# Decoder layer on one core: the last values projection, the first turns, the last mergings and a gate tile change places in TensorE's order

## What is computed

```python
x = layernorm(x + self_attn(x))           # 32 heads of 16, causal, with biases
x = layernorm(x + cross_attn(x, ctx))     # 32 query heads of 128, 8 key/value heads, rotary q and k
x = layernorm(x + ffn(x))                 # silu(x Wg) * (x Wu), then Wd; 4-bit weights, 1376 wide
```

```python
q = rope(heads(query @ wq)); k = rope(heads(ctx @ wk)); v = heads(ctx @ wv)
w = softmax(mask(q k^T / sqrt(128)))      # 4 query heads share one k/v head
out = merge_heads(w v) @ wo
```

## Time and profile before

| what | value |
|---|---|
| median of three runs | 888.88 us (887.12 to 889.69) |
| the profiled execution: its time | 887.8 us |
| the profiled execution: its span, first to last instruction | 885.9 us |
| mean granted clock of TensorE in it | 0.993 |
| TensorE busy | 95% of the span |
| VectorE busy | 82% of the span |

### The profile page before, as it was taken

How to read it: one execution, slowest core, us unless ns; L and a number is a source line. 1 busy time by engine, 2 the same in 40 slices (tenths; PEclk the granted TensorE clock), 3 DMA queues, 4 the chain that set the end, 5 groups by cost and what they waited for, 6 DMA issues and landing times.

```text
span 885.9 us, 17326 instructions
## 1 busy us (share of the span) xinstructions
PE 841.4 (95%) x6141; PEld 470.2 (53%) x6141; DVE 726.9 (82%) x1129; ACT 497.2 (56%) x1487; POOL 590.0 (67%) x522
## 2 busy tenths in 40 slices
PE   8898999889799999999999999999999899999897
PEld 4666777555445555555555555554555544333343
DVE  5589998877777888879788788798899764899887
ACT  5787889443555555556565565654654652777400
POOL 1264449886647775776677677578788642887885
PEclk9999999999999999999999999999999999999999
DMA  6765245203134413314224215113622412330011
GB/s 181 232 202 161 73 132 163 66 1 120 25 90 126 107 36 85 86 46 132 61 37 120 61 36 153 38 25 87 141 74 41 101 31 71 96 129 3 1 48 47
DMA packets 119893, 76.75 MB, mean 87 GB/s; under 512 B 72861, under 2 KB 104064, under 8 KB 119808
## 3 DMA queue, kind: packets, MB, share of 16 engines
q1 hardware_dynamic: 117504, 74.99, 31.3%
q10 hardware_dynamic: 2304, 0.66, 0.3%
HBM read 52.50 MB, written 6.36 MB: 66 GB/s over the span
## 4 chain that ended last, share of the span: by engine, by line
PE 51%; POOL 15%; DVE 14%; issue 7%; ACT 7%; DMA 4%; SPq 0%; ACTq 0%; DVEq 0%; POOLq 0%
PE bank L359 14%; PE bank L360 14%; PE bank L361 14%; POOL rot L630 3%; DVE total L1305 2%; DMA pT<-pn 2%; POOL pn L647 2%; POOL q2l L636 2%; ACT prob L807 1%; ACT prob L946 1%; DVE rsin L1169 1%; POOL deq L659 1%; DVE nmax L1090 1%; POOL left L663 1%; PE bank L1545 1%
## 5 line engine op out<-in xcount | busy, mean ns | idle before, releaser
L640 POOL TENSOR_TENSOR prob<-prob,rden 128x512 f32<-128x512 f32 x64 | 66.7, 1041 | 124.6 <-DVE rden L1234 124.6
L630 POOL TENSOR_TENSOR rot<-rcos,rsin 128x512 f32<-128x512 f32 x80 | 106.6, 1332 | 19.4 <-DVE rsin L1169 19.3
L359 PE MATMUL bank<-aTh,xqh 128*128 128x512 f16 x256 | 97.0, 379 | 3.5 <-DVE aTl L1059 2.4
L359 PE MATMUL bank<-xoh,o2h 128*128 128x512 f16 x256 | 97.5, 381 | 0.0
L360 PE MATMUL bank<-xol,o2h 128*128 128x512 f16 x256 | 97.3, 380 | 0.0
L361 PE MATMUL bank<-xoh,o2l 128*128 128x512 f16 x256 | 97.3, 380 | 0.0
L361 PE MATMUL bank<-aTh,xql 128*128 128x512 f16 x256 | 97.0, 379 | 0.0
L360 PE MATMUL bank<-aTl,xqh 128*128 128x512 f16 x256 | 97.0, 379 | 0.0
L946 ACT ACTIVATE prob<-bank,ebias 128x128 f32<-128x128 f32 x256 | 90.6, 366 | 2.1
L1169 DVE SCALAR_TENSOR_TENSOR rsin<-bank,sinq 64x512 f32<-64x512 f32 x128 | 88.1, 688 | 1.7
L636 POOL TENSOR_TENSOR q2l<-rot,q2h 128x512 f16<-128x512 f32 x64 | 82.2, 1284 | 4.4 <-ACT q2h L843 4.4
(11 more groups left out here) (212 smaller groups left out, 2626.9 us busy)
## 6 DMA issues: line engine op xcount, KB each, us to landing
tst<-tables SPq DMA_DIRECT2D x11, 768.0 KB, 6.1
xqs<-in_xwq SPq DMA_DIRECT2D x8, 1024.0 KB, 7.2
xos<-in_xwo SPq DMA_DIRECT2D x8, 1024.0 KB, 5.5
qst<-in_fq SPq DMA_DIRECT2D x11, 384.0 KB, 3.4
kstk<-stack SPq DMA_DIRECT2D x48, 64.0 KB, 2.3
qstk<-stack SPq DMA_DIRECT2D x21, 128.0 KB, 2.6
xs<-in_ctxT SPq DMA_DIRECT2D x2, 1024.0 KB, 7.7
res<-in_x SPq DMA_DIRECT2D x1, 2048.0 KB, 8.2
```

Of the source, the lines that this page charges most:

```text
L359: pe.matmul(out_ap, ah, bh, start=first, stop=False)
L630: nc.gpsimd.tensor_tensor(rot[:, r % 2, :], rcos[:, r % 2, :], rsin[:, r % 2, :], ALU.add).then_inc(rope_rot, 1)
L640: nc.gpsimd.tensor_tensor(prob[:, v % 2, :].rearrange("p (h k) -> p h k", h=QH), prob[:, v % 2, :].rearrange("p (h k) -> p h k", h=QH), rd ...
```

## The change

In the plan of fills the values of block 15 go from END - 4 to END - 5, turn 0 from END - 6 to END - 5, behind them; turns 1, 2 and 3 keep END - 5, END - 4 and END - 3. The place of the values in the list goes from 113 to 111, of turn 0 from 111 to 112, of turn 1 from 112 to 113. So step END - 5 has three fills: the values ahead of weigh, turns 0 and 1 behind it and ahead of merge. VectorE and ScalarE take the same order from the list. At step END + 1 merge(62) goes ahead of weigh(63). At END + 2 the gate tile 2 goes ahead of merge(63); its up tile stays behind the late turn. Nothing is added or left out.

```diff
-                 (s + 3, "q", (block, 3)), (s + 3 if block < len(ORDER) - 1 else s + 5, "v", (block,))]
-    plan += [(END - 6 + b, "t", (1, b)) for b in range(4)]
+                 (s + 3, "q", (block, 3)), (s + 3 if block < len(ORDER) - 1 else s + 4, "v", (block,))]
+    plan += [(END - 5, "t", (1, 0)), (END - 5, "t", (1, 1)), (END - 4, "t", (1, 2)), (END - 3, "t", (1, 3))]
...
-EARLY_GU = {END - 2: [0], END: [1], END + 2: [2], END + 4: [3]}
+EARLY_GU = {END - 2: 0, END: 1, END + 2: 2, END + 4: 3}
...
-            def gate_up(n):
+            def gate_or_up(n, m):
...
                 for f in fills_at(t)[:1]:
                     fill(f)
+                if v == STEPS + 1:
+                    merge(v - 3)
+                if v == STEPS + 2:
+                    gate_or_up(EARLY_GU[t], 0)
                 if 2 <= v <= STEPS + 1:
                     weigh(v - 2)
                 for f in fills_at(t)[1:]:
                     fill(f)
-                if 3 <= v <= STEPS + 2:
+                if 3 <= v <= STEPS + 2 and v != STEPS + 1:
                     merge(v - 3)
                 if t in LATE_TURN:
                     late_turn(LATE_TURN[t])
-                for n in EARLY_GU.get(t, ()):
-                    gate_up(n)
+                if t in EARLY_GU:
+                    if v != STEPS + 2:
+                        gate_or_up(EARLY_GU[t], 0)
+                    gate_or_up(EARLY_GU[t], 1)
```

More of the change, by code:

```diff
@@ L1677, in merge @@
                 last.then_inc(c_wo, 1)
-            def gate_up(n):
+            def gate_or_up(n, m):
                 i, half = GATE_UP[n]
[L1681 to L1691, removed]
+                if m == 0:
+                    pe.wait_ge(f_wlo, i + 1)
+                    if n == 0:
+                        pe.wait_ge(fill_free, NF)
+                    if n == 1:
+                        pe.wait_ge(c_exp, STEPS)
+                    if n in (2, 3):
+                        pe.wait_ge(f_inter, n - 1)
+                project(bank[2 * (n % 2) + m][:, :], [wgh[i][:, m, k * P:(k + 1) * P] for k in range(NK)],
+                        [wgl[i][:, m, k * P:(k + 1) * P] for k in range(NK)], aTh, aTl,
+                        slice(half * HALF, (half + 1) * HALF)).then_inc((f_gate, f_up)[m], 1)
             def bank_free(c, p):
```

## The result

| | before | changed |
|---|---|---|
| median | 888.88 us (887.12 to 889.69, six runs) | 892.82 us (890.46 to 893.57, six runs) |
| ratio, 95% interval | | 1.0037 (1.0023 to 1.0051) |
| profiled execution: time, span | 887.8, 885.9 us | 890.46, 888.5 us |

The kernel is slower by 3.3 us by the ratio (2.0 to 4.5), 3.9 by the medians. I had said 891.2 and a range of 889.2 to 892.9. The median lies in the range by 0.08 us only, and the loss is larger than the 2.3 us forecast. (The median before is now of six executions; three of them were known when the prediction was made.)

What follows compares the result with a forecast made beforehand. TensorE, busy 95% of the span, was taken as the bound, so its waits and slow clock count. Turn 3's 0.90, slow clock 0.9 and last steps 0.5 gave +2.3 us: 888.88 to 891.2 us, range 889.2 to 892.9.

Steps and rivals of the forecast that it cites:

- The stall: Step END - 5, before turn 1: TensorE stands still 4.18 us until the values' low part is copied.
- The values fill: Ahead of weigh(57): its 2.68 us lie wholly in time in which TensorE waited before.
- The work from turn 1 to turn 3: TensorE's turns, mergings, scores and weigh(58) from turn 1 to turn 3 take 8.47 us together.
- The lateness of turn 3: Turn 3 is late by 1.8 us and this reaches weigh(62) in full, through VectorE, ScalarE and GpSimd.
- rival C: Ahead of weigh(62) the lateness is swallowed; only part 2's 0.5 us stays, 889.4 us; chance 0.13.
- The turn of batch 6: In the last steps this turn waits 0.53 us for the norm of batch 6.
- Rival A: Before turn 1 the new wait is short, so the kernel is not slower: 886.1 us; chance 0.12.
- the slow clock behind the new wait: TensorE's lower clock after the wait before turn 1 costs 0.9 us, between 0 and 1.7.
- 0.90: Sum up to turn 3 without slow clock: turn 3 starts at 706.91 against 706.01, +0.90 us.
- Rival B: The slow clock behind the new wait is paid in full, 1.46 us: total +2.9, 891.8 us; chance 0.25.
- D: The last norms lie on the path: 2.6 us instead of 0.5, total +4.4, 893.3 us; chance 0.10.
- the likeliest case: The forecast itself, over both parts: +2.3 us, 891.2 us, own range 889.8 to 892.0; chance 0.40.

Runs made afterwards that it cites:

- e5: The changed kernel with 16 extra matmuls between turns 0 and 1, their sum thrown away; ratio 1.0012 to the kernel before.
- e2: The kernel before with only the change's last steps, plan of fills as before; ratio 1.0012 to the kernel before.
- e4: The changed kernel with merge(56) ahead of turns 0 and 1 in step END - 5; ratio 0.9999 to the kernel before.
- e8: As e4, but with the last steps as in the kernel before; ratio 0.9984 to the kernel before.
- e6: The changed kernel with the values' copies moved up in ScalarE's and VectorE's streams; ratio 1.0004 to the kernel before.
- e1: The kernel before with only the change's plan of fills, last steps as before; ratio 1.0033 to the kernel before.
- e9: The changed kernel with turn 1 at END - 4, load of codes and tables 5 after tile 58's transpose, last steps as before; 887.62 us, ratio 0.9981.
- e11: The kernel before with only the load of codes and tables 5 moved behind tile 58's transpose; ratio 1.0004 to the kernel before.

## Why the prediction was right, and the one term that was too small

**The steps that held.** Counted from weigh(57), the prediction had turn 1 at +5.26 (698.44 - 693.18); measured +5.32. The stall was to be 4.18 us between starts; between turn 0's start plus 0.43 and turn 1 it was 4.24 (692.83 to 697.50 less 0.43). The values fill cost nothing, hidden by the DMA wait of weigh(57), 1.77 left of it. The work from turn 1 to turn 3 was to be 8.47 us at the full clock; e5 measured 8.53. The lateness of turn 3 reached weigh(62) undiminished (+3.05 and +3.05), as ScalarE's idle time in the chain had said, so rival C falls. A further 0.30 that weigh(60) lost to its late probabilities was taken up, as said, by the wait ahead of weigh(62), 1.28 instead of 1.58. The turn of batch 6 was to wait 0.53 us; 747.74 less 746.78 + 0.43 is 0.53, and so is the difference behind weigh(62) between e2 and the kernel before and between e4 and e8. Rival A fell where it said it would be decided: turn 1 started at 697.50, which is 698.50 on the scale of the kernel before, and not by 696.1.

**The term that was mis-sized** is the slow clock behind the new wait. The text put it between 0 and 1.7 us and took 0.9; it is 2.03, outside its own bounds. The upper bound came from the one fall that the trace of before showed, 3.4 us long, half of which can be lost. The new fall lasted twice as long, 6.8 us: 2.7 of it lay inside the wait and cost nothing, the other 4.1 lay over turn 1 and merge(56), and 2.03 is about half of that. A bound drawn from the length of a single instance isn't a bound. With 2.03 in place of 0.9 the sum is 0.90 + 2.03 + 0.53 = +3.46, against 3.58 in the trace and 3.3 in the ratio; the missing 0.12 is 0.06 in the start of turn 1 and 0.06 in the 8.47. Rival B, which took 1.46 for it and put the median at 891.8, was the nearest of the cases in its mechanism, though it too stayed below 2.03. The median by itself lies nearer to D's 893.3, whose cause e2 refutes. That the median is inside the range owes something to luck: the likeliest case's own range ended at 892.0, and the last tenths up to 892.9 had been added partly for D.

The rule of the Trainium skill (TensorE: Matmul & The Clock Gate, section "HAM oscillation — how this bites in real kernels") ties a fall of the clock to one long unbroken idle gap. The trace agrees for the new wait of 4.07 us, in which the fall began. The falls in the kernel before and in e6, behind two shorter waits with a little work between, are not covered by that rule, and e4, with a merging between two such waits, had none.

**The median** lies 0.5 us above what +3.46 on 888.88 gives. The profiled execution was the fastest of the six, and the other executions' mean granted clock was 0.989 to 0.993 against its 0.993. So more or longer falls of the clock may make part of the spread, here or at other places; that stays open, as only one execution was profiled.

## What to carry to other kernels

Before putting several bank-using fills into one step, look at what takes each out of its bank and where that stands in its own engine's stream: a third fill with two banks waits for the first one's copies, and all ready work behind it on TensorE waits too. Put work with operands at hand (here a merging) ahead of what waits, and cost a wait of TensorE with the lower clock behind it. And when a stall goes, name the next wait at each place: here a DMA transpose made slow by a bulk load issued ahead of it on the same queue, which nothing had to wait for until then.

## What the runs showed of the hardware that was not expected

- In a wait of 4.07 us TensorE's granted clock fell to half and stayed there until 4.1 us after its work had begun again; 16 filler matmuls in the wait kept it at full and were worth 2.03 us. e1, with the same wait, lost 2.32 to the slow clock.
- Two waits of 1.74 and 1.73 us with 1.1 us of matmuls between brought a fall (e6); waits of 1.75 and 1.50 us with 3.7 us of matmuls between brought none (e4).
- A DMA transpose of 256 KB that takes 3.05 us alone took 5.54 us beside a load of 1.1 MB. That the load is the cause is shown by moving it: with it issued later the same transpose took 3.1 us (e9), and the next one, then behind the load, 5.0 (e11).
